# Attention of a gated layer: scores with tokens on the partitions, means and weight sums as extra columns, quads in a new order, and the first choice of tokens at six places of a quad

## The chip, the cores and the metric

One core of one Trainium2 chip runs the whole program. The metric is the device time of one execution in microseconds (us); lower is better. Tokens are handled in tiles of 128, one token per partition; a quad is four tiles (512 tokens), and there are 8 quads, q = 0 to 7, four for each of the two sequences of the batch (b = 0 and 1).

## What is computed

The reference, cut to its core (x is 2 x 2048 x 512, the context 2 x 77 x 512, 8 experts, each takes k = 512 tokens of each sequence, hidden size 2048, everything float32):

```python
xn = layernorm(x)
q, k, v = xn @ Wq.T + bq, ctx @ Wk.T + bk, ctx @ Wv.T + bv
attn = softmax(where(mask == 0, -inf, q @ k.T / sqrt(512)))
x = x + tanh(g_xattn) * (attn @ v @ Wo.T + bo)
xn = layernorm(x)
probs = softmax(xn @ gate_w.T)            # per token, over 8 experts
g, m = top_k(probs.transpose(0, 2, 1), k) # per sequence and expert
h = gelu(xn[m] @ w1) @ w2                 # per expert
x = x + tanh(g_ffn) * scatter_add(g * h)
```

## The kernel before

The program is written out per engine, with counting semaphores between the engines; each engine runs its own list in order, so the order of the code is the order of the work. It has four parts.

**Weights folded** (`prep_pe`, `prep_out`). Keys times Wq, the mean of each column taken off, become `qkc`, with 77 score columns and 8 router columns (JE = 85) per sequence; values times Wo become `vo` (77 x 512) and, times the router, `vg` (77 x 8). Part 0 is what the scores need, part 1 the rest.

**Attention, quad by quad** (`attention_pe`, `attention_act`, `attention_pool`, `attention_dve`). For a quad PE transposes the four tiles of x (L552), ACT copies them out as `xT` (L641), PE multiplies `qkc` (stationary, 85 columns) with `xT` (512 columns moving) into scores with the tokens on the free axis (L572), ACT copies them out as `sT` (L661), and PE turns them back so that tokens are on the partitions (L602). DVE scales and adds the mask bias (L793, four instructions), copies the router columns (L798), takes the largest score (L800) and its negative (L801). ACT takes four exponentials, whose row sums come out by its accumulator (L670). PE transposes them (L561), ACT copies them out as `eT` (L649). PE multiplies `eT` with `vo` (L590) and `vg` (L592), tile by tile, in turn. DVE multiplies by the reciprocal row sum (L764) and adds x (L770, "weigh"), then takes mean and variance of the new row (L817, L820), and POOL normalizes (L692 to L739). `logits_out` (L751 to L755) forms the router's logits. The spread of x comes from DVE for the first three quads, later from ACT: sum, mean, squares (L616, L620, L627). The quads overlap by one: in iteration `it`, PE does the transposes of x and the scores of quad `it`, and the rest of quad `it - 1`; DVE puts the score work of quad `it` between the second and the third weigh of quad `it - 1`.

**Choice** of 512 of 2048 tokens per expert, by a search over the bits of the threshold (`choice_dve`, `choice_pe`): 10 pieces of the same kind, each of which gets the counts of the piece before from PE (L886, L890), makes seven new thresholds (L895) and compares all probabilities with them (L899), after which PE counts (L962); then a piece for what lies above and at the threshold (L912 to L923), and a piece for the places (L930 to L942). Piece 0 also forms the probabilities. For b = 0 the function `between` lays the pieces beside the attention. Before, it does so from iteration `CHOOSE_FROM` = 5 on, at 3 places per iteration; all that is left runs in iteration 8. Then come `hot_dve` and `slots_dve` (L1366 to L1386) and `slots_pe` (L1355), which give the rows to fetch, POOL fetches them (L1419), PE transposes them (L1437), and ACT and DVE split them in two parts (L1442, L1452).

**Experts.** Expert 0 is plain (`hidden_pe` L1185, `output_pe` L1325); beside its first sequence DVE runs the second choice (b = 1). The other seven run products in a seven-product form (L1211). This part is the same in both kernels.

```python
        CHOOSE_FROM, PLACES = QB + 1, 3
...
            def between(it, place):
                at = (it - CHOOSE_FROM) * PLACES + place
                if it == NQ and place > 0:
                    pieces = range(at, N_PIECES) if place == 1 else ()
                else:
                    pieces = range(at, at + 1) if 0 <= at < N_PIECES else ()
```

## Time and profile before

| | us |
|---|---|
| three runs: median (lowest to highest) | 1578.08 (1573.19 to 1578.4) |
| the profiled execution: its time | 1578.86 |
| the profiled execution: its span | 1577.1 |
| first matmul of expert 0 (L1185), from the span's start | 183.18 |
| PE busy over the span | 1498.4 (95%) |
| DVE busy over the span | 1023.2 (65%) |

The profile's first part gives busy time per engine, the second cuts the span into 40 slices. In the first seven slices (0 to 276 us) PE is at 6 to 8 tenths, and after them at 9 and more. The chain that ended last is on PE for 85% of the span; the views by stage and by instruction, below, are of the part that lies ahead of the experts.

### The profile page before, as it was taken

How to read it: one execution, taken by the hardware profiler on the slowest of the kernel's cores; microseconds unless marked ns; L12 is line 12 of the kernel's file. 1: busy time of each engine (PE TensorE's matmuls, PEld its weight loads, DVE VectorE, ACT ScalarE, POOL GpSimd, SP SyncE). 2: the span in 40 equal slices, each digit the busy share in tenths (PEclk: the TensorE clock that was granted, in tenths of full speed). 3: DMA queues.
4: the chain of work that ended last, by engine and by line, in shares of the span. 5: the costliest groups of instructions: out<-in, count | busy, mean ns of one | idle time of the engine just before them, and what ended most of it. 6: DMA issues, size and time to landing. Idle time of an engine off the chain costs nothing.

```text
span 1577.1 us, 22321 instructions
## 1 busy us (share of the span) xinstructions
PE 1498.4 (95%) x7169; PEld 1214.6 (77%) x7169; DVE 1023.2 (65%) x1729; ACT 733.6 (47%) x1347; POOL 574.8 (36%) x541
## 2 busy tenths in 40 slices
PE   6887688999999999999999999999999999999996
PEld 5654467787788888888888888888888888888885
DVE  2578777557766767575766667667667665766642
ACT  1384233345444544455445454455445444554432
POOL 2266512453453144432443144404432344323311
PEclk9998799999999999999999999999999999999999
DMA  6175522553432443244323424244334423342133
GB/s 227 59 259 191 161 79 64 137 154 89 90 96 80 94 107 100 89 87 102 107 85 83 110 79 127 57 105 90 99 93 87 115 81 107 81 107 81 40 81 67
DMA packets 101401, 163.58 MB, mean 104 GB/s; under 512 B 7411, under 2 KB 45315, under 8 KB 101285
## 3 DMA queue, kind: packets, MB, share of 16 engines
q1 hardware_dynamic: 86885, 128.50, 26.1%
q0 software_dynamic: 14400, 33.56, 11.5%
q8 instruction: 69, 1.13, 0.3%
q14 instruction: 47, 0.39, 0.1%
HBM read 128.48 MB, written 33.55 MB: 103 GB/s over the span
## 4 chain that ended last, share of the span: by engine, by line
PE 85%; DVE 8%; ACT 2%; issue 2%; POOL 1%; DMA 1%; POOLq 0%; SPq 0%; DVEq 0%; ACTq 0%
PE bank L1325 42%; PE bank L1211 33%; PE bank L1185 4%; PE bank L1480 1%; PE bank L572 1%; PE bank L590 1%; DVE w2hl L1170 1%; PE bank L400 1%; DVE count L852 1%; DVE st L817 1%; DVE onehot L1366 1%; DVE atleast L899 1%; ACT xT L641 1%; DVE sc L793 0%; PE bank L1355 0%
## 5 line engine op out<-in xcount | busy, mean ns | idle before, releaser
L1325 PE MATMUL bank<-w2hl,hh 128*128 128x512 f32 x2048 | 637.8, 393 | 0.0
L1211 PE MATMUL bank<-xo,whl 128*128 128x512 f32 x2352 | 545.1, 390 | 4.8 <-DVE mix L1275 2.8
L1211 PEld LDWEIGHTS bank<-xo,whl 128*128 128x128 f32 x2352 | 441.8, 188 | 100.3 <-DVE mix L1275 3.7
L1325 PEld LDWEIGHTS bank<-w2hl,hh 128*128 128x128 f32 x2048 | 381.7, 189 | 76.5
L1325 PE MATMUL bank<-w2hl,hid_low 128*128 128x512 f32 x1024 | 399.8, 390 | 0.0
L1325 PEld LDWEIGHTS bank<-w2hl,hid_low 128*128 128x128 f32 x1024 | 192.8, 188 | 40.4
L1430 POOL DMA_INDIRECT layer_out<-y,slot_row x64 | 102.8, 1606 | 302.1 <-ACT y L1345 287.3
L1170 DVE TENSOR_TENSOR w2hl<-raw,w2hl 128x512 fp32r<-128x512 f32 x226 | 160.5, 731 | 53.0 <-ACT w2hl L1165 44.1
L1139 POOL TENSOR_TENSOR whl<-raw,whl 128x512 fp32r<-128x512 f32 x56 | 81.6, 1456 | 262.1 <-ACT whl L1105 262.1
L1165 ACT ACTIVATE w2hl<-raw 128x512 fp32r<-128x512 f32 x228 | 136.6, 625 | 58.1 <-DMA raw<-in_L_ffn_w 39.4
L1144 POOL TENSOR_TENSOR whl<-wsum,whl 128x512 fp32r<-128x512 f32 x56 | 75.1, 1340 | 183.6 <-ACT whl L1126 183.6
L1250 ACT ACTIVATE mix<-bank 128x512 f32<-128x512 f32 x56 | 33.3, 595 | 199.7 <-PE bank L1211 199.3
L1257 ACT ACTIVATE hid<-bank 128x512 f32<-128x512 f32 x56 | 33.5, 598 | 158.0 <-PE bank L1211 158.0
L1278 DVE TENSOR_TENSOR mix<-bank,mix 128x512 f32<-128x512 f32 x56 | 38.7, 692 | 101.3 <-PE bank L1211 99.3
L1185 PE MATMUL bank<-xp,whl 128*128 128x512 f32 x384 | 94.7, 397 | 1.7 <-DVE xp L1452 1.7
L1303 DVE TENSOR_TENSOR hid_low<-hid,hh 128x512 fp32r<-128x512 f32 x112 | 86.5, 778 | 12.8 <-ACT hh L1298 12.8
L1275 DVE TENSOR_TENSOR mix<-bank,mix 128x512 f32<-128x512 f32 x56 | 38.5, 688 | 80.8 <-PE bank L1211 80.5
L1185 PEld LDWEIGHTS bank<-xp,whl 128*128 128x128 f32 x384 | 73.6, 192 | 18.1 <-DVE xp L1452 2.4
L1133 POOL TENSOR_TENSOR whl<-raw,whl 128x512 fp32r<-128x512 f32 x32 | 46.9, 1485 | 105.9 <-ACT whl L1101 105.9
L1291 DVE TENSOR_TENSOR hid_low<-hid,hh 128x512 fp32r<-128x512 f32 x112 | 79.9, 713 | 0.5 <-ACT hh L1266 0.4
L1283 DVE TENSOR_TENSOR hid<-bank,mix 128x512 f32<-128x512 f32 x56 | 38.7, 691 | 63.5 <-PE bank L1211 63.4
L1146 POOL TENSOR_TENSOR whl<-wsum,whl 128x512 fp32r<-128x512 f32 x56 | 76.4, 1364 | 0.0
(224 smaller groups left out, 1771.8 us busy)
## 6 DMA issues: line engine op xcount, KB each, us to landing
raw<-in_L_ffn_w SPq DMA_DIRECT2D x228, 256.0 KB, 2.7
raw<-in_L_ffn_w SPq DMA_DIRECT2D x72, 512.0 KB, 4.8
x_s<-in_x SPq DMA_DIRECT2D x8, 1024.0 KB, 7.0
layer_out<-x SPq DMA_DIRECT2D x8, 1024.0 KB, 8.9
xn_rows<-xn SPq DMA_DIRECT2D x8, 1024.0 KB, 4.8
raw_k<-in_L_xattn_Wk SPq DMA_DIRECT2D x1, 1024.0 KB, 5.1
raw_q<-in_L_xattn_Wq SPq DMA_DIRECT2D x1, 1024.0 KB, 11.2
raw_v<-in_L_xattn_Wv SPq DMA_DIRECT2D x1, 1024.0 KB, 13.4
```

What stands on the lines that cost most here:

```text
L1133: last = pool.tensor_tensor(low[:, 4 * half:4 * half + 4, :].rearrange("p i f -> p (i f)"), raw1[:, p % 2, 2 * half:2 * half + 2, :].rearr ...
L1139: pool.tensor_tensor(low[:, 2 * A11:2 * A11 + 4, :], raw1[:, p % 2, :, 0:P], high[:, 2 * A11:2 * A11 + 4, :], ALU.subtract)
L1144: pool.tensor_tensor(low[:, 2 * S1:2 * S1 + 4, :], wsum[:, 0:4, :], high[:, 2 * S1:2 * S1 + 4, :], ALU.subtract)
L1146: pool.tensor_tensor(low[:, 2 * S3:2 * S3 + 4, :], wsum[:, 4:8, :], high[:, 2 * S3:2 * S3 + 4, :], ALU.subtract).then_inc(w1_low, 1)
L1165: act.activation(w2hl[:, f % 4, HIGH, :], raw2[:, slot, :], ACT.Copy).then_inc(w2_high, 1)
L1170: eng.tensor_tensor(w2hl[:, f % 4, LOW, :], raw2[:, slot, :], w2hl[:, f % 4, HIGH, :].bitcast(F32), ALU.subtract).then_inc(w2_low_early if ...
L1185: last = pe.matmul(H_BANKS[f % 2][:, :], whl[:, p % 2, part, 2 * k + f % 2, :], xp[:, b, xpart, k, :], start=(k == 0 and part == HIGH and ...
L1211: last = pe.matmul(bk[:, :], whl[:, p % 2, part, 2 * w + k, :], xo[:, xpart, x, k, :], start=(not adds and k == 0 and part == HIGH and xpa ...
L1291: dve.tensor_tensor(hid0_low[:, f % 4, :], hid0[:, f % 4, :], hh[:, f % 4, :].bitcast(F32), ALU.subtract)\
L1303: dve.tensor_tensor(hid1_low[:, f, :], hid1[:, f, :], hh[:, s % 4, :].bitcast(F32), ALU.subtract)\
L1325: last = pe.matmul(Y_BANKS[c][:, :], high if hpart == HIGH else low[:, c * P:(c + 1) * P], w2hl[:, f % 4, part, :], start=(s == 0 and hpar ...
L1430: pool.indirect_dma_start(out_rows, bass.IndirectOffsetOnAxis(ap=slot_row[:, b, c:c + 1], axis=0), y[:, c, :], None, compute_op=ALU.add).t ...
```

## The change

Scores: `score` takes `xT` of a tile as the stationary operand and `qkc` as the moving one, so that tokens come out on the partitions; `sT`, its copy and its turn back go. `qkc` gets an 86th column of -1/512, whose product is minus the mean of x (`xg1[..., E]`), and ACT's sums and `xmean` go; `vg` gets a ninth column of ones, whose product is the row sum of the exponentials, and the reciprocal is taken from that. DVE subtracts the largest score itself (`sm`), and ACT takes one exponential per quad. The banks for transposed tiles are two, before three; those for scores two, before one.

Order: per quad q, PE does the scores of quad q + 1 around the turn of the exponentials of q, then `route`, four `weigh_pe`, and the transposes of x of quad q + 2. DVE finishes quad q before it begins the score work of q + 1. The choice begins with quad 4 (`CHOOSE_FROM` = 4), with 6 places per quad; `hot_dve` and `slots_dve` are pieces 12 and 13. POOL fetches the first rows ahead of its work on quad 6.

```diff
-        T_BANKS = (2, 3, 4)
+        T_BANKS = (2, 3)
         O_BANKS = (bank[0], bank[1])
-        CHOOSE_FROM, PLACES = QB + 1, 3
+        SC_BANKS = (bank[6], bank[4])
+        CHOOSE_FROM, PLACES = QB, 6
...
+        def score(pe, q, i):
+            if i == 0:
+                wait(pe, mean_ready, q - 1)
+                wait(pe, sc_ready, q - 1)
+            pe.wait_ge(turn_out, turn_at["x", q, i] + 1)
+            for k in range(KD):
+                last = pe.matmul(SC_BANKS[q % 2][:, i * JM:(i + 1) * JM], xT[:, q % 2, k, i * P:(i + 1) * P],
+                                 qkc[:, k, q // QB, :], start=(k == 0), stop=(k == KD - 1))
+            if i == Q - 1:
+                last.then_inc(scored, 1)
+        def turn_e(pe, q):
+            pe.wait_ge(exped, q + 1)
...
+        def route(pe, q):
+            pe.wait_ge(turn_out, turn_at["e", q, 0] + 1)
+            wait(pe, rinv_ready, q)
+            for i in range(Q):
+                last = pe.matmul(VG_BANK[:, i * EM:(i + 1) * EM], eT[:, q % 2, i * P:(i + 1) * P], vg[:, q // QB, :],
+                                 start=True, stop=True)
+            last.then_inc(routed, 1)
+        def weigh_pe(pe, q, i):
+            n = Q * q + i
+            wait(pe, added, n - 1)
+            pe.matmul(O_BANKS[n % 2][:, :], eT[:, q % 2, i * P:(i + 1) * P], vo[:, q // QB, :],
+                      start=True, stop=True).then_inc(weighed, 1)
...
+            for q in range(NQ):
+                if q + 1 < NQ:
+                    score(pe, q + 1, 0)
+                    between(q - 1, 5)
+                    score(pe, q + 1, 1)
+                turn_e(pe, q)
+                if q + 1 < NQ:
+                    score(pe, q + 1, 2)
+                    score(pe, q + 1, 3)
+                between(q, 0)
+                route(pe, q)
+                weigh_pe(pe, q, 0)
+                weigh_pe(pe, q, 1)
+                between(q, 1)
+                weigh_pe(pe, q, 2)
+                between(q, 2)
+                weigh_pe(pe, q, 3)
+                for i in range(Q):
+                    if q + 2 < NQ:
+                        turn_x(pe, q + 2, i)
+                    if i == 0:
+                        between(q, 3)
+                    if i == 2:
+                        between(q, 4)
...
+            for q in range(NQ):
+                exps(q)
+                e_out(q)
+                if q == CHOOSE_FROM:
+                    choice_act(act, 0)
+                if LEAD <= q + 1 < NQ:
                     for i in range(Q):
+                        square(q + 1, i)
+                if q + 2 < NQ:
                     for i in range(Q):
+                        x_out(q + 2, i)
...
-                if it == NQ:
-                    w1_low_pool(pool, 0, 0, 0)
+                if it == NQ - 1:
                     for c in range(NC):
                         gather_pool(pool, 0, 0, c)
+                if it == NQ:
                     promote_pool(pool, 0, 0)
+                    w1_low_pool(pool, 0, 0, 0)
...
+            router_in(0)
+            prep_out(dve, prep_dve, False, 1, own)
+            for q in range(NQ):
+                softmax_in(q)
+                if q >= 1:
+                    logits_out(q - 1)
+                if q == CHOOSE_FROM:
+                    choice_start_dve(dve, own, 0)
+                if q + 1 < NQ:
+                    router_in(q + 1)
+                between(q, 0)
+                weights_in(q)
+                weigh(q, 0)
+                between(q, 1)
+                weigh(q, 1)
+                weigh(q, 2)
+                between(q, 2)
+                weigh(q, 3)
+                stats(q, (0,))
+                between(q, 3)
+                stats(q, (1, 2))
+                between(q, 4)
+                stats(q, (3,))
+                moments(q)
+                between(q, 5)
+            for c in range(NC):
                 split_tokens_dve(dve, 0, c)
             logits_out(NQ - 1)
...
+            def between(q, place):
+                at = (q - CHOOSE_FROM) * PLACES + place
+                if 0 <= at < N_PIECES + 2:
+                    do(at)
+            return between
```

`softmax_in` is the four instructions with the mask bias, the largest score and the subtraction, after waits for the scores, for POOL's factor and for the bias; `router_in` copies the nine columns out; `weights_in` copies the router's part out and takes the reciprocal of the ninth column.

The program's order of instructions shows two places. The first is DVE in a quad without a piece of the choice, from the first weigh on. Before (`sc` are the masked scores, `st` and `mv` the statistics of the new rows, `lg` the logits' steps):

```order
L770 SCALAR_TENSOR_TENSOR x<-bank,rinv,x_s 128x512 x2
L793 SCALAR_TENSOR_TENSOR sc<-bank,norm,mbias 128x77 x4
L798 COPY xg<-bank 128x32
L800 TENSOR_REDUCE smax<-sc 128x4
L801 TENSOR_SCALAR smaxn<-smax 128x4
L770 SCALAR_TENSOR_TENSOR x<-bank,rinv,x_s 128x512 x2
L817 BN_STATS st<-x 128x6 x4
L820 BN_AGGR mv<-st 128x2 x4
```

And in the changed program:

```order
L798 SCALAR_TENSOR_TENSOR x<-bank,rinv,x_s 128x512 x4
L807 BN_STATS st<-x 128x6 x4
L812 BN_AGGR mv<-st 128x2 x4
L752 SCALAR_TENSOR_TENSOR sc<-bank,norm,mbias 128x77 x4
L758 TENSOR_REDUCE smax<-sc 128x4
L760 TENSOR_TENSOR sm<-sc,smax 128x308
L775 TENSOR_TENSOR lg<-lgv,rinv 128x32
L777 TENSOR_TENSOR lg<-lg,xg 128x32
L779 TENSOR_TENSOR logits<-lg,norm 128x32
L769 COPY xg<-bank 128x36
L786 COPY lgv<-bank 128x32
L787 RECIPROCAL rinv<-bank 128x4
```

The score work of the next quad stood between the second and the third weigh; now it stands behind the statistics, and right ahead of the same quad's weigh.

The second place is PE in quad 4 of the changed program, from the second half of the scores of quad 5 on (L976 counts for the choice, L575 is `route`, L582 `weigh_pe`, L547 the transposes of x of quad 6):

```order
L558 MATMUL bank<-qkc,xT 128x86 x8
L976 MATMUL bank<-atleast,ones_m 128x56 x16
L575 MATMUL bank<-vg,eT 128x9 x4
L582 MATMUL bank<-vo,eT 128x512 x2
L976 MATMUL bank<-atleast,ones_m 128x56 x16
L582 MATMUL bank<-vo,eT 128x512
L976 MATMUL bank<-atleast,ones_m 128x56 x16
L582 MATMUL bank<-vo,eT 128x512
L547 MATMUL bank<-ident,x_s 128x128 x4
L976 MATMUL bank<-atleast,ones_m 128x56 x16
```

And DVE in the same quad, from the end of piece 0 to the last weigh:

```order
L913 TENSOR_TENSOR atleast<-prob,cand 128x896
L786 COPY lgv<-bank 128x32
L787 RECIPROCAL rinv<-bank 128x4
L798 SCALAR_TENSOR_TENSOR x<-bank,rinv,x_s 128x512
...
L913 TENSOR_TENSOR atleast<-prob,cand 128x896
L798 SCALAR_TENSOR_TENSOR x<-bank,rinv,x_s 128x512 x2
...
L913 TENSOR_TENSOR atleast<-prob,cand 128x896
L798 SCALAR_TENSOR_TENSOR x<-bank,rinv,x_s 128x512
```

Three counts of the choice now stand on PE ahead of `route`, of the third and of the fourth weigh of the same quad, and each waits for a comparison (`atleast`) on DVE; before, an iteration had one count ahead of the third weigh, one ahead of the transposed exponentials and one within the scores.

## Rows read from the trace of the kernel before

**Rows 1.** Busy time by engine, share of the span, instructions.

```profile
PE 1498.4 (95%) x7169; PEld 1214.6 (77%) x7169; DVE 1023.2 (65%) x1729; ACT 733.6 (47%) x1347; POOL 574.8 (36%) x541
```

**Rows 2.** Busy time per engine in stretches; last but two, PE's granted clock.

```profile
56.10:183.20 127.10, 93.92 (x581) 55.57 (x579) 92.23 (x257) 66.66 (x195) 67.67 (x94) 0.89 0.56 187
...
57.00:104.00 47.00, 42.99 (x196) 24.37 (x195) 28.71 (x82) 31.97 (x101) 24.04 (x36) 1.00 0.59 198
...
120.00:140.00 20.00, 16.35 (x121) 8.73 (x120) 17.49 (x51) 13.62 (x41) 12.96 (x17) 1.00 0.67 233
140.00:160.00 20.00, 12.49 (x98) 8.00 (x97) 16.44 (x40) 4.43 (x13) 13.06 (x16) 0.74 0.41 152
160.00:180.00 20.00, 6.62 (x69) 4.79 (x67) 13.64 (x39) 2.25 (x3) 6.48 (x11) 0.66 0.52 164
```

**Rows 3.** Timeline, DVE, at 56 us: start, us, engine, line, [idle before <-releaser].

```profile
55.94 0.17 DVE L460 COPY vg<-bank 77x16 f32<-77x16 f32 x1 [0.36 <-PE bank L432]
```

**Rows 4.** Timeline, DVE, one quad without choice.

```profile
98.40 0.75 DVE L770 SCALAR_TENSOR_TENSOR x<-bank,rinv,x_s 128x512 f32<-128x512 f32 x1 [1.95 <-PE bank L590]
...
100.05 0.90 DVE L793 SCALAR_TENSOR_TENSOR sc<-bank,norm,mbias 128x77 f32<-128x77 f32 x4
...
101.21 0.47 DVE L800 TENSOR_REDUCE smax<-sc 128x4 f32<-128x308 f32 x1
...
103.11 2.46 DVE L817 BATCH_NORM_STATS2 st<-x 128x6 f32<-128x512 f32 x4
105.61 0.38 DVE L820 BATCH_NORM_AGGREGATE mv<-st 128x2 f32<-128x6 f32 x4
```

**Rows 5.** Timeline, PE and ACT, from one quad to another two later.

```profile
70.08 0.59 ACT L649 ACTIVATE eT<-bank 77x512 f32<-77x512 f32 x1
...
92.80 0.63 PE L561 MATMUL bank<-ident,ex 128*77 128x128 f32 x4
93.50 0.59 ACT L649 ACTIVATE eT<-bank 77x512 f32<-77x512 f32 x1
93.76 3.63 PE L572 MATMUL bank<-xT,qkc 128*85 128x512 f32 x8 [0.34 <-ACT xT L641]
...
97.24 1.02 PE L590 MATMUL bank<-vo,eT 128*128 128x512 f32 x2
98.09 0.28 PE L592 MATMUL bank<-vg,eT 128*128 128x8 f32 x2
```

**Rows 6.** Timeline, PE: small matmuls with loads of 128 and of 77 columns.

```profile
42.19 4.44 PE L400 MATMUL bank<-ctxT,wvT 128*128 128x154 f32 x32 [1.45 <-ACT wvT L455]
...
54.69 1.21 PE L432 MATMUL bank<-qkc,voT 128*77 128x8 f32 x16
```

**Rows 7.** Timeline, ACT and DVE: exponential and subtraction of 128 columns.

```profile
108.78 0.29 DVE L864 TENSOR_TENSOR prob<-logits,pstat 128x128 f32<-128x128 f32 x1
...
109.11 0.31 ACT L856 ACTIVATE pexp<-prob 128x128 f32<-128x128 f32 x1 [3.31 <-DVE prob L864]
```

**Rows 8.** Timeline: a piece of the choice on DVE, then PE's count.

```profile
131.74 0.20 DVE L886 SCALAR_TENSOR_TENSOR found<-bank,cand 128x56 f32<-128x56 f32 x1
...
133.53 2.46 DVE L817 BATCH_NORM_STATS2 st<-x 128x6 f32<-128x512 f32 x4
133.67 0.59 PE L962 MATMUL bank<-atleast,ones_m 128*128 128x56 bf16 x16 [0.47 <-DVE atleast L899]
```

**Rows 9.** Timeline, DVE: the first choice's end.

```profile
162.37 0.21 DVE L886 SCALAR_TENSOR_TENSOR found<-bank,cand 128x56 f32<-128x56 f32 x1
...
167.70 2.29 DVE L1366 TENSOR_TENSOR onehot<-iota_slot,slot_lo 128x2048 bf16<-128x2048 bf16 x1
```

**Rows 10.** Timeline: PE at half clock, first fetch, first matmul of expert 0.

```profile
154.23 2.05 PE L590 MATMUL bank<-vo,eT 128*128 128x512 f32 x2 [0.33 <-issue]
...
172.77 1.14 POOL L1419 DMA_INDIRECT xg<-xn_rows,next_row  x1 [12.26 <-DVE next_row L1386]
...
183.18 6.17 PE L1185 MATMUL bank<-xp,whl 128*128 128x512 f32 x18 [1.72 <-DVE xp L1452]
```

More of the change, by code:

```diff
@@ L512, in prep_out @@
                 elif name == "vg":
[L513 removed]
+                    last = copy(vg[0:J, :, 0:E], bk[0:J, 0:B * E].rearrange("p (b e) -> p b e", b=B))
                 last.then_inc(mine, 1)
@@ L516, in prep_out @@
                     lead_stats_dve(eng, own, LEAD_AT[name, i])
-        turns = []
-        for it in range(NQ + 1):
-            turns += [("x", it, i) for i in range(Q) if it < NQ]
-            turns += [("e", it - 1, 0)] if it >= 1 else []
-            turns += [("s", it, 0)] if it < NQ else []
+        turns = [("x", q, i) for q in range(2) for i in range(Q)]
+        for q in range(NQ):
+            turns += [("e", q, 0)]
+            turns += [("x", q + 2, i) for i in range(Q) if q + 2 < NQ]
@@ new lines, in pe_bank_free, with turn_x @@
+            wait(pe, turn_out, turn_at[turn] - 1)
+        def turn_x(pe, q, i):
+            if i == 0:
+                pe.wait_ge(x_in[q % 3], 16 * (q // 3 + 1))
+            pe_bank_free(pe, ("x", q, i))
+            for k in range(KD):
+                last = pe.transpose(turn_bank(("x", q, i))[:, k * P:(k + 1) * P],
+                                    x_s[:, q % 3, i, k * P:(k + 1) * P], ident[:, :])
+            last.then_inc(turned, 1)
+        def score(pe, q, i):
[3 more added lines that the diff above has]
+            pe.wait_ge(turn_out, turn_at["x", q, i] + 1)
+            for k in range(KD):
+                last = pe.matmul(SC_BANKS[q % 2][:, i * JM:(i + 1) * JM], xT[:, q % 2, k, i * P:(i + 1) * P],
+                                 qkc[:, k, q // QB, :], start=(k == 0), stop=(k == KD - 1))
+            if i == Q - 1:
+                last.then_inc(scored, 1)
@@ L679, in first_deviations @@
                 s = q % 2
+                wait(pool, sc_ready, q - 1)
                 if q < LEAD:
@@ L824, in attention_dve, with stats, moments @@
-            for c in (0, 1):
+            def stats(q, tiles):
+                if tiles[0] == 0 and q >= 1:
+                    dve.wait_ge(x1_stats, q)
+                for i in tiles:
+                    dve.wait_ge(added, Q * q + i + 1)
+                    own.mark(dve.bn_stats(st2[:, i, :], x1[:, q % 2, i, :]))
+            def moments(q):
+                dve.wait_ge(dve_own, own.n)
+                for i in range(Q):
+                    last = dve.bn_aggr(mv2[:, q % 2, i, :], st2[:, i, :])
+                    own.mark(last) if i < Q - 1 else last.then_inc(x1_stats, 1)
@@ new lines, in attention_dve @@
+            router_in(0)
+            prep_out(dve, prep_dve, False, 1, own)
+            for q in range(NQ):
+                softmax_in(q)
[20 more added lines that the diff above has]
+                between(q, 5)
@@ L870, in step @@
                 dve.wait_ge(dve_own, own.n)
-            if b == 0 and piece == 0:
-                choice_start_dve(dve, own, 0)
             if piece == 0:
@@ L978, in beside_attention, with first_choice_dve, do, first_choice_pe @@
         def beside_attention(do):
-            def between(it, place):
-                at = (it - CHOOSE_FROM) * PLACES + place
-                if it == NQ and place > 0:
-                    pieces = range(at, N_PIECES) if place == 1 else ()
-                else:
-                    pieces = range(at, at + 1) if 0 <= at < N_PIECES else ()
-                for piece in pieces:
-                    do(0, piece)
-            return between
+            def between(q, place):
[3 more added lines that the diff above has]
+            return between
+        def first_choice_dve(dve, own):
+            def do(piece):
+                if piece < N_PIECES:
+                    choice_dve(dve, own, 0, piece)
+                elif piece == N_PIECES:
+                    hot_dve(dve, 0, 0)
+                else:
+                    slots_dve(dve, 0, 0)
+            return do
+        def first_choice_pe(pe):
+            def do(piece):
+                if piece < N_PIECES:
+                    choice_pe(pe, 0, piece)
+                elif piece == N_PIECES:
+                    slots_pe(pe, 0)
+            return do
         H_BANKS = (bank[4], bank[5])
@@ L1825, in _ @@
             pool.memset(mean_m[:, :], 1.0 / D).then_inc(consts, 1)
+            for b in range(B):
+                pool.memset(qkc[:, :, b, JE:JM], -1.0 / D).then_inc(tails, 1)
+                pool.memset(vg[:, b, E:EM], 1.0).then_inc(tails, 1)
             pool.wait_ge(pool_start, 4)
@@ L1857, in _ @@
             attention_act(act)
-            act.wait_ge(scored, NQ)
+            for c in range(NC):
+                first_tokens_act(act, c)
             for f in range(2):
@@ L1862, in _ @@
             w1_high_act(act, 0, 0, 1)
-            for c in range(NC):
-                first_tokens_act(act, c)
             choice_act(act, 1)
```

320 lines of the change are left out of this document (113 added, 207 removed).

## The prediction

> **What bounds the kernel now.** I read the busy times first: PE works 95% of the span [rows 1], and the experts, where it is full, are the same program in both kernels. So only the time from the start to the first matmul of expert 0, at 183.18 us [rows 10], can change, and whatever moves that matmul moves the end by as much. Next the stretches: from 56.1 to 183.2 us PE is busy 93.92 of 127.1 us and DVE 92.23 [rows 2]; neither is full. In the quads without choice PE is nearly so (42.99 of 47 us), and the work repeats every 11.7 us: the transposed exponentials are copied out at 70.08 and, two quads later, at 93.50 [rows 5]. From quad 4 on DVE has three pieces of the choice to a quad, and after 140 us PE falls to 12.49 and 6.62 of 20 us and is granted its faster clock only for part of it [rows 2]. So what counts is how the engines wait for one another, and I follow one quad after the other through the new order, by durations of the trace. I take 0.05 us from one engine's end to the next one's start, and from the start of a `vo` product to the DVE work on it 1.14 us (97.24 to 98.40, and 0.86 us of it is PE's own time) [rows 4, 5].
>
> **Start.** The folding of the weights is the same work. The changed PE does the first scores and the second quad's transposes ahead of part 1 instead of behind it, and waited there for copies anyway; I leave its end at 56.1 us, where DVE copies `vg` [rows 3]. PE's work up to there counts at nothing because those waits cover it; if they don't, it costs up to 2 us.
>
> **A quad without choice, before 11.7 us.** I set t = 0 where DVE begins `softmax_in`.
> - DVE: the masked scores take 0.90, the largest 0.47 [rows 4]. The subtraction of 308 elements isn't in the trace; it lies between the same with 128 elements, 0.29 [rows 7], and a 512-element weigh, 0.75 [rows 4]; I take 0.48. With the gaps DVE is through at 1.96.
> - ACT: one exponential of 308, between 0.31 for 128 [rows 7] and 0.59 for 512 [rows 5]; 0.46, to 2.46. PE turns from 2.5; ACT's copy starts 0.70 after PE, as in [rows 5], and ends at 3.8.
> - PE in the meantime does two tiles of the next quad's scores, 16 instructions with 128 columns loaded and 86 moved. They are bounded by 0.076 us each (8 columns moved, 77 loaded) and by 0.139 (154 moved, 128 loaded) [rows 6]; the loads are full size, so I take 0.12, 0.95 a tile. PE is free at 4.85. All four tiles cost 3.8 against 3.63 before [rows 5]; only the turn back and the copy of `sT` are saved. `route` is 8 more such instructions, to 5.8.
> - DVE weighs at 6.94 (5.8 + 1.14) and 7.9; the third product needs the first bank, so it is weighed at about 8.96, the fourth at 9.84, to 10.6. Then 2.46 and 0.38 for the statistics [rows 4]: 13.4.
> This chain passes DVE, ACT, PE, ACT, PE and DVE again with nothing put beside it, because the score work of the next quad no longer stands between two weighs. ACT and POOL are busy for about half of the stretch, 66.66 and 67.67 of 127.1 us [rows 2], and ACT for less after the change; its saved sums and three exponentials count at nothing, since it waits in any case. A quad costs 13.4 for 11.7.
>
> At the scores the Trainium skill has a rule ("TensorE: Matmul & The Clock Gate", "LDWEIGHTS (loading the stationary operand)"): a load takes its columns divided by 1.2 nanoseconds, 107 ns for 128, however few columns then move. It speaks against this change, which now loads 128 columns for every 86. By it the two tiles that stand in the chain would take 1.7 us in place of my 1.9 and the sum would be 1 us less over the quads; the trace's 0.139 us with 128 columns is near it.
>
> **A quad with six pieces.** A piece is 1.8 us on DVE (131.74 to 133.53), a count 0.6 on PE [rows 8]. Quad 4:
> - To 2.6 as above, with `logits_out`, then the choice's start; `router_in` must wait for the scores, 5.2. Piece 0 with its probabilities is 2.2 us, to 7.5. PE counts to 8.2, and only then does `route`, to 9.15: DVE waits until 10.3 for the first weigh, 11.05.
> - Piece 1 to 12.85, second weigh to 13.55. PE was free, but its third product stands behind the count of piece 1, from 13.5: weighed at 14.65, to 15.35.
> - Piece 2 to 17.15; count, fourth product from 17.8: weighed at 18.95. DVE waits 1.8 us with nothing to do. To 19.65.
> - Statistics and pieces 3, 4 and 5 follow without a wait: 28.0.
> Quad 5 the same, with pieces 6 to 9, then 5.3 us for the last two, 162.37 to 167.70 [rows 9]: 29.1. Quad 6: the one-hot matrices (`hot_dve`, 2.29 us [rows 9] and two small ones, 3.0) are ahead of `slots_pe` and `route`: first weigh at 10.9, end at 17.8. POOL fetches from 12.3 on, while the quad goes on. Before, expert 0 began 10.4 us after the first fetch, at 172.77 [rows 10]; that latency is now hidden. Quad 7 has no scores behind the exponentials: weighed from 5.9, statistics to 12.3; then four splits, of which the last two wait for two banks (PE, ACT, DVE in turn), 15.9. There expert 0 begins.
>
> **Sum.** 56.1 + 4 x 13.4 + 28.0 + 29.1 + 17.8 + 15.9 = 200.5, against 183.2: 17.3 us later. DVE's own work in it is about 98 us (92.23, and 6 for subtraction, copies and the moved first scores), so it would wait 46 of 144 us, where before it waited 35 of 127.
>
> **PE's clock.** Before, PE was granted 0.74 of full speed where it was busy 12.49 of 20 us, and 0.66 where 6.62 [rows 2]; at the half clock (1.2 GHz) a `vo` product of 1.02 us took 2.05 [rows 10]. In quads 4 and 5 of my walk PE is busy 14 of 28 us, in pieces with pauses of up to 3 us. In its chain stand, per quad, turn and scores 2.3, `route` 0.95, three products 2.6 and about 1 for the counts: nearly 7 us, that double at the half clock; 5 in quad 6. So this costs between 0 and 19 us. As the pauses are shorter than those of before, I take a third, 6 us.
>
> 17.3 + 6 = 23 us. The profiled execution took 1578.86 us (0.8 over the median of the runs): 1578.9 + 23 = 1602 us.
>
> **The rivals.**
> - The half clock holds through the choice. For it: the pauses recur four times a quad. Against it: from 120 to 140 us, with PE busy 16.35 of 20 us and choice pieces beside it, the clock stayed full [rows 2]. Price 19 in place of 6: 1615 us. The Trainium skill has this as a rule (same page, "HAM oscillation — how this bites in real kernels"): a program that pauses between short bursts begins every burst slow. By that, this rival would be the forecast.
> - Slower by little: full clock, score matmuls at 0.076 us each (0.7 us off the chain in eight places), a quicker handing over. 17.3 less 6 gives 11 us: 1590.
> - No change: the loss in quads 0 to 3 (6.8 us) stays, but the choice loses nothing, because its pieces fill DVE's waits. What DVE waits in quads 4 and 5 (about 7 us each) would have to go. 1582 us.
> - Faster: DVE, not the chain, sets the time. It decides as soon as DVE's waits from 56 us on fall under 29 us (127.1 - 98). One quad's pieces would have to run while PE is in the turn and the products of the same quad. If DVE never waited, expert 0 would begin at 154 and the time be 1550; halfway to my walk's 200.5 it is 1573. For it: 35 us of idle DVE time exist, and the fetch is hidden. Against it: the order of PE has three counts ahead of three products of the same quad, and PE's matmuls keep their order.
>
> **How the numbers follow.** A measurement here tells about 0.5% from no change, 7.9 us. The forecast (some loss of clock, 1592 to 1610) 0.50; half clock, 1610 and more, 0.20; slower by little 0.15; no change 0.08; faster 0.07. So slower 0.85, same 0.08, faster 0.07. The range takes the first and the third case whole and the half clock to 1620: 1586 to 1620.
>
> **What would show it.** Right: in the changed profile DVE's first weighs of quads 1, 2 and 3 are 13 to 14 us apart, in quads 4 and 5 about 28; DVE waits 1 to 2 us for PE at the third and the fourth weigh of these; the first matmul of expert 0 lies at 200 us or later, and behind it the distances are as before. Wrong: quads without choice at 12 us or less, or choice quads under 24 us, or that matmul before 183 us. A clock of 1.00 from 110 to 190 us would take the 6 us away, one near 0.5 would give the first rival.

## The result, and the profile after

The changed kernel took 1620.68 us, the median of 4 runs (1619.94 to 1621.75); the kernel before 1576.49 us, the median of its 4 (1573.19 to 1578.4). The ratio is 1.0287, with a 95% interval of 1.0266 to 1.0307: slower, as forecast, but by 44 us in place of 23, and 0.7 us outside the range. The profiled execution took 1620.17 us with a span of 1618.3; before, 1578.86 and 1577.1.

The first part of the changed kernel's page, against [rows 1]:

```profile
PE 1523.5 (94%) x7329; PEld 1246.7 (77%) x7329; DVE 1028.0 (64%) x1738; ACT 709.6 (44%) x1238; POOL 568.9 (35%) x545
```

The span grew by 41.2 us. Where it grew is read from the first and last start of one line's matmuls. In the answer for the plain product of expert 0 (L1205 now, L1185 before) and the one for the seven-product form (L1231 now, L1211 before), the two numbers behind the comma are those starts; first before, then after:

```profile
L1185 PE MATMUL bank<-xp,whl x384: 387/389/796, 183.2 to 380.4; 128*128 128x512 f32 x192
L1211 PE MATMUL bank<-xo,whl x2352: 387/389/628, 383.5 to 1510.3; 128*128 128x512 f32 x196
```

```profile
L1205 PE MATMUL bank<-xp,whl x384: 388/389/796, 219.1 to 417.4; 128*128 128x512 f32 x192
L1231 PE MATMUL bank<-xo,whl x2352: 387/389/636, 420.6 to 1551.5; 128*128 128x512 f32 x196
```

Expert 0 begins 35.9 us later (219.1 for 183.2), the second expert 37.1 later, and the last matmul of L1231 41.2 later. So 36 us were lost ahead of the experts, and 5.3 in a part that is the same in both kernels. The first loss is 18.6 us more than the walk of the prediction gave it, the second was not in it at all.

The quads of the changed kernel, cut where DVE begins `softmax_in`; the last stretch ends with the first matmul of expert 0 (us, the busy time of PE, PEld, DVE, ACT and POOL with its count, last but two the granted clock):

```profile
55.44:68.61 13.17, 11.98 (x81) 9.21 (x80) 8.01 (x22) 3.23 (x6) 2.04 (x2) 1.00 0.09 18
68.61:86.36 17.75, 15.51 (x70) 11.68 (x70) 8.49 (x27) 3.23 (x6) 8.07 (x12) 0.71 0.51 175
86.36:99.50 13.14, 10.81 (x70) 8.03 (x70) 8.48 (x26) 6.16 (x14) 7.86 (x12) 1.00 0.49 180
99.50:117.16 17.66, 15.41 (x70) 11.60 (x70) 8.47 (x27) 6.16 (x14) 8.17 (x13) 0.71 0.69 219
117.16:147.77 30.61, 18.17 (x143) 12.60 (x143) 20.10 (x54) 6.57 (x15) 9.56 (x15) 0.75 0.51 167
147.77:178.44 30.67, 22.43 (x193) 17.10 (x192) 20.14 (x61) 6.37 (x14) 8.51 (x13) 0.69 0.25 89
178.44:199.80 21.36, 12.37 (x54) 8.39 (x53) 11.73 (x32) 3.98 (x10) 8.09 (x11) 0.68 0.24 71
199.80:219.10 19.30, 11.26 (x37) 6.57 (x37) 10.93 (x30) 5.09 (x9) 10.63 (x19) 0.70 0.70 248
```

Quads 0 and 2 ran at a full clock and took 13.17 and 13.14 us, where the walk had 13.4. Quads 1 and 3 hold the same work (70 matmuls each in quads 1, 2 and 3), were granted 0.71 of the clock and took 17.75 and 17.66. So the order costs 1.5 us a quad against the 11.7 of before, and the clock 4.5 more in every second one. Quads 4 and 5 took 30.6 and 30.7 for the walk's 28.0 and 29.1, quad 6 took 21.4 for 17.8, and the last stretch 19.3 for 15.9.

The timeline of DVE in quad 1, from the copy of the router columns to the last weigh, and then the same in quad 2:

```profile
75.64 0.20 DVE L769 COPY xg<-bank 128x36 f32<-128x36 f32 x1 [4.50 <-PE bank L558]
77.22 0.19 DVE L786 COPY lgv<-bank 128x32 f32<-128x32 f32 x1 [1.38 <-PE bank L575]
...
79.22 0.75 DVE L798 SCALAR_TENSOR_TENSOR x<-bank,rinv,x_s 128x512 f32<-128x512 f32 x1 [1.72 <-PE bank L582]
80.83 0.75 DVE L798 SCALAR_TENSOR_TENSOR x<-bank,rinv,x_s 128x512 f32<-128x512 f32 x1 [0.86 <-PE bank L582]
...
91.32 0.20 DVE L769 COPY xg<-bank 128x36 f32<-128x36 f32 x1 [2.43 <-PE bank L558]
92.15 0.19 DVE L786 COPY lgv<-bank 128x32 f32<-128x32 f32 x1 [0.63 <-PE bank L575]
...
93.21 1.51 DVE L798 SCALAR_TENSOR_TENSOR x<-bank,rinv,x_s 128x512 f32<-128x512 f32 x2 [0.78 <-PE bank L582]
```

Each wait of DVE for PE about doubles: 4.50 for 2.43, 1.38 for 0.63, 1.72 for 0.78. They are the links of the chain that the prediction named (turn, scores, `route`, product), and with nothing beside them DVE pays PE's slower pace in full.

In quad 4, DVE at the third and fourth weigh (L798), and PE's counts (L976) of the same quad:

```profile
133.35 0.75 DVE L798 SCALAR_TENSOR_TENSOR x<-bank,rinv,x_s 128x512 f32<-128x512 f32 x1 [1.28 <-PE bank L582]
138.80 0.75 DVE L798 SCALAR_TENSOR_TENSOR x<-bank,rinv,x_s 128x512 f32<-128x512 f32 x1 [2.89 <-PE bank L582]
```

```profile
131.47 0.59 PE L976 MATMUL bank<-atleast,ones_m 128*128 128x56 bf16 x16 [1.85 <-DVE atleast L913]
131.89 1.42 PE L582 MATMUL bank<-vo,eT 128*128 128x512 f32 x2
135.96 0.93 PE L976 MATMUL bank<-atleast,ones_m 128*128 128x56 bf16 x16 [2.65 <-DVE atleast L913]
136.71 2.05 PE L582 MATMUL bank<-vo,eT 128*128 128x512 f32 x2
```

The two engines take turns: PE waits 2.65 us for DVE's comparison with a product behind it that was ready, then DVE waits 2.89 for the product. The last product came at the half clock (2.05 us for two instructions), so the 1.8 us foreseen at the fourth weigh became 2.9.

What PE waited for over the whole span (engine, line, <- releaser: us, times, longest), the first rows of the changed kernel:

```profile
PE bank L976 <- DVE atleast L913: 18.6, 9, 2.6
PE bank L567 <- ACT ex L644: 17.2, 7, 6.0
...
PE bank L1231 <- issue: 4.9, 4, 1.3
```

Before, the corresponding wait for comparisons was 10.0 us in 6 and a wait for exponentials was not among the rows; the row with "issue" had no counterpart either. It stands in the experts' loop:

```profile
764.90 1.75 PE L1231 MATMUL bank<-xo,whl 128*128 128x512 f32 x7
767.77 4.40 PE L1231 MATMUL bank<-xo,whl 128*128 128x512 f32 x18 [1.12 <-issue]
```

PE does seven matmuls of a pass of the loop and then stands still for 1.12 us, with no semaphore to wait for. This happens four times, 4.9 us in all, and they cover what this line lost: of the 5.3 us, 4.1 lie between the first and the last start of this line (1130.9 us for 1126.8), and the other 1.2 in expert 0.

### The profile page after: what moved, and what is told of

Same layout as the page of the kernel before. It is cut to its first block, busy times and chain, and to the rows that moved or that the text cites. A ratio compares the mean times of both kernels' runs of the same rounds, so it can differ in the third digit from the quotient of the medians.

```text
span 1618.3 us, 22526 instructions
## 1 busy us (share of the span) xinstructions
PE 1523.5 (94%) x7329; PEld 1246.7 (77%) x7329; DVE 1028.0 (64%) x1738; ACT 709.6 (44%) x1238; POOL 568.9 (35%) x545
## 4 chain that ended last, share of the span: by engine, by line
PE 85%; DVE 9%; issue 2%; ACT 2%; DMA 1%; POOL 0%; POOLq 0%; SPq 0%; DVEq 0%; ACTq 0%
PE bank L1345 40%; PE bank L1231 32%; PE bank L1205 3%; PE bank L582 2%; PE bank L1502 1%; PE bank L558 1%; DVE st L807 1%; DVE atleast L913 1%; DVE w2hl L1190 1%; PE bank L399 1%; DVE count L868 1%; PE bank L575 1%; DVE onehot L1386 1%; DVE cand L909 0%; PE bank L567 0%
## 5 line engine op out<-in xcount | busy, mean ns | idle before, releaser
L1231 PE MATMUL bank<-xo,whl 128*128 128x512 f32 x2352 | 545.5, 390 | 8.4 <-issue 4.9
L1231 PEld LDWEIGHTS bank<-xo,whl 128*128 128x128 f32 x2352 | 441.2, 188 | 104.8 <-issue 8.2
L1185 ACT ACTIVATE w2hl<-raw 128x512 fp32r<-128x512 f32 x228 | 136.4, 624 | 58.7 <-DMA raw<-in_L_ffn_w 41.7
L1277 ACT ACTIVATE hid<-bank 128x512 f32<-128x512 f32 x56 | 33.5, 598 | 163.7 <-PE bank L1231 163.7
L1205 PE MATMUL bank<-xp,whl 128*128 128x512 f32 x384 | 96.3, 402 | 1.4 <-DVE xp L1474 1.4
L1205 PEld LDWEIGHTS bank<-xp,whl 128*128 128x128 f32 x384 | 74.6, 195 | 17.5 <-DVE xp L1474 1.7
## 6 DMA issues: line engine op xcount, KB each, us to landing
raw_v<-in_L_xattn_Wv SPq DMA_DIRECT2D x1, 1024.0 KB, 13.4
```

What stands on the lines that cost most here:

```text
L1185: act.activation(w2hl[:, f % 4, HIGH, :], raw2[:, slot, :], ACT.Copy).then_inc(w2_high, 1)
L1205: last = pe.matmul(H_BANKS[f % 2][:, :], whl[:, p % 2, part, 2 * k + f % 2, :], xp[:, b, xpart, k, :], start=(k == 0 and part == HIGH and ...
L1231: last = pe.matmul(bk[:, :], whl[:, p % 2, part, 2 * w + k, :], xo[:, xpart, x, k, :], start=(not adds and k == 0 and part == HIGH and xpa ...
```

## The experiments

**Theories.** A, the order on PE: counts ahead of ready products, and no softmax work between weighs, make a chain that nothing covers. B, the clock: the chain would be bearable if PE kept 2.4 GHz. C, six places or the early start of the choice are at fault by themselves. D, the stop in the experts comes from where the loop lies in PE's program. The kernel before took 1575.53 us beside the first four runs and 1575.92 beside the next four. "Front" below is the first matmul of expert 0, "rest" the span from there to its end: 183.2 and 1393.9 before, 219.1 and 1399.2 after. Front and rest come from one profiled execution each, and each time but the last two is a single run.

The front also holds the folding of the weights, which most edits leave alone and which still ends at different times: the 32 matmuls at 15 to 16 us took 6.50 us in the change and 4.44 with the counts behind, and no trace here says why. So the table counts the attention from a mark that all kernels have, the start of DVE's copy of `vg` [rows 3]; the walk had 144.6 us from there.

| kernel | `vg` copied | expert 0 | between | rest |
|---|---|---|---|---|
| before | 55.9 | 183.2 | 127.2 | 1393.9 |
| the change | 55.3 | 219.1 | 163.7 | 1399.2 |
| counts behind | 52.7 | 197.4 | 144.7 | 1399.3 |
| softmax between | 54.0 | 203.8 | 149.8 | 1399.0 |
| both | 55.6 | 181.2 | 125.5 | 1398.2 |
| idle matmuls | 53.2 | 201.9 | 148.7 | 1394.4 |
| three places | 55.2 | 222.0 | 166.8 | 1396.5 |
| eight small matmuls | 55.4 | 218.9 | 163.5 | 1392.7 |
| late softmax, idle matmuls | 53.4 | 194.5 | 141.1 | 1390.5 |
| late softmax | 55.8 | 180.0 | 124.2 | 1390.9 |
| the same again | 53.2 | 177.8 | 124.6 | 1393.9 |
| scores first | 55.6 | 180.9 | 125.4 | 1391.8 |

**Counts behind the products (A).** PE's first three counts of a quad each go behind the product that they stood ahead of.

```diff
-                between(q, 0)
                 route(pe, q)
                 weigh_pe(pe, q, 0)
                 weigh_pe(pe, q, 1)
+                between(q, 0)
+                weigh_pe(pe, q, 2)
                 between(q, 1)
-                weigh_pe(pe, q, 2)
+                weigh_pe(pe, q, 3)
                 between(q, 2)
-                weigh_pe(pe, q, 3)
```

> The changed kernel with one thing else: in PE's list each count of the choice at the places 0, 1 and 2 stands behind the product that it stood ahead of. Theory (order and clock): DVE no longer waits at the first, third and fourth weigh of quads 4 and 5; by the walk at full clock this is 5.2 us in each of the two and 2 in quad 6, 12 us, and some 8 more because PE's part of the chain there also ran at half clock: first matmul of expert 0 at about 200 in place of 219.7 us, time about 1600. Rival (the places of the counts don't matter, DVE waits for something else): no change, 1620.

Measured 1598.77 us: 22 less than the change. The front is at 197.4, the rest 1399.3. From the mark it is 19.0 us less: that is what three places a quad had on PE ahead of the products cost, half of the 36.5 us lost there.

**Softmax work between two weighs (A).** `softmax_in` of quad q + 1 moves from behind the statistics to between the second and the third weigh of quad q, the place that it had in the kernel before.

```diff
-            for q in range(NQ):
-                softmax_in(q)
+            softmax_in(0)
+            for q in range(NQ):
...
                 weigh(q, 1)
+                if q + 1 < NQ:
+                    softmax_in(q + 1)
                 weigh(q, 2)
```

> The changed kernel with DVE's four score instructions, largest score and subtraction of quad q + 1 put back between the second and the third weigh of quad q, where they stood before. Theory: the chain DVE, ACT, PE, ACT, PE of a quad again runs beside the statistics of the quad before; quads 0 to 3, now 61.7 us together, take about 47 (11.7 each), and PE keeps the full clock there; 15 to 25 us in all, time 1595 to 1605. Rival (the new form of the scores costs by itself, not the order): quads stay at 13 and more, time above 1612.

Measured 1604.64: 16 less. The front is at 203.8, the rest 1399.0. The quads without choice now take 11.6 to 13.1 us (ends of the statistics at 73.15, 84.72, 97.81 and 110.88), not the 11.7 expected: `softmax_in` stands ahead of the third weigh, and there DVE waited 2.54 us for POOL's factor and, a quad later, 2.87. From the mark the edit gives 14 us.

**Both (A).** The two edits together.

> Both edits of order together: counts behind the products, score work of the next quad between two weighs. Theory: DVE becomes the bound of quads 4 and 5 (about 20 us each), quads without choice take 11 to 12 us; expert 0 begins at 175 to 185 us, time 1575 to 1585, so about the kernel before. If the six places were the fault in themselves, it would stay above 1600.

Measured 1581.38. The front is at 181.2, 2 us ahead of the kernel before; the rest is 1398.2, with the stops in the loop (3.7 us in 4). From the mark the two edits alone gave 19 and 14, which add to 33, and together they gave 38.2. So the order accounts for all of the 36.5 that was lost ahead of the experts. The granted clock from 100 to 180 us was only 0.81, with DVE busy most of the time:

```profile
100.00:180.00 80.00, 57.47 (x450) 41.13 (x447) 65.48 (x179) 22.77 (x50) 41.95 (x61) 0.81 0.55 181
```

DVE is busy 65.48 of 80 us in it; in the kernel before it was 64.26. That the clock matters little when DVE is this full is argued; no run holds the clock in this order.

**Idle matmuls that keep the clock (B).** Ahead of each turn of the exponentials PE does six matmuls whose result is overwritten, and ahead of each count eight. The order of the change stays.

```diff
+        def warm(pe, bk, n):
+            for _ in range(n):
+                pe.matmul(bk[:, 0:P], ident[:, :], mean_m[:, :], start=True, stop=True)
...
+                pe_bank_free(pe, ("e", q, 0))
+                warm(pe, turn_bank(("e", q, 0)), 6)
                 turn_e(pe, q)
```

> The changed kernel with idle matmuls added on PE where it waits (6 of 128 x 128 ahead of each turn of the exponentials, 8 ahead of each count of the choice), whose results nobody reads. Theory (the half clock is what the walk at full clock lacks): granted clock 1.00 nearly throughout from 56 to 200 us, quads 0 to 3 at 13.2 us each, expert 0 begins at about 201 in place of 219.7, time about 1601. Rival (the clock is a symptom, the waits come from elsewhere): time 1620 or, with the matmuls in the way, more.

Measured 1598.33: 22 less. Stretches of it:

```profile
56.00:100.00 44.00, 41.13 (x275) 32.08 (x275) 25.96 (x76) 14.88 (x32) 19.82 (x31) 1.00 0.56 177
100.00:160.00 60.00, 53.43 (x509) 44.67 (x508) 42.08 (x106) 15.54 (x36) 21.15 (x30) 1.00 0.48 157
160.00:180.00 20.00, 18.67 (x165) 15.34 (x164) 12.85 (x42) 4.58 (x11) 8.10 (x12) 0.91 0.20 69
```

The clock is full to 160 us, all of quads 1 to 3 take 13.15 us (ends of the statistics at 66.91, 80.05, 93.20, 106.35), and the front is at 201.9. From the mark that is 15 us less than the change. With the 38.2 of the order that makes 53, more than the 36.5 there are: in part they are the same microseconds, since a chain that is covered does not feel the clock. In this kernel PE does not stop in the loop, and its rest is 1394.4.

The idle matmuls did not hold the clock to the end. The last stretch, from the `softmax_in` of quad 7 to expert 0, is as long as in the change (19.05 for 19.30 us):

```profile
182.85:201.90 19.05, 11.02 (x36) 6.72 (x36) 10.98 (x30) 5.05 (x9) 10.99 (x19) 0.74 0.68 236
```

So the full-clock walk is tested up to there: it had 128.5 us from the first `softmax_in` to that of quad 7, and this kernel took 129.5, the change 144.4.

**The choice as before, three places from quad 5 on (C).** The pieces run at places 1, 3 and 4 of quads 5 to 7, the remaining ones behind quad 7, and the fetch behind them, as in the kernel before; all else is the change.

```diff
-        CHOOSE_FROM, PLACES = QB, 6
+        CHOOSE_FROM, PLACES = QB + 1, 3
...
+                elif q >= CHOOSE_FROM and place in (1, 3, 4):
+                    do((q - CHOOSE_FROM) * PLACES + (1, 3, 4).index(place))
```

> The changed kernel with the six places undone: the choice begins with quad 5, three pieces per quad (behind the first weigh, and between the statistics), the last three search pieces (9 and on), one-hot matrices and fetch behind quad 7, as before the change. Theory: six places are not the fault in themselves. Quads 5 to 7 get about 19, 19 and 17 us, the tail 21: at full clock 200 us to expert 0, the same as with six places, with the same loss of clock 212 to 222 us; time 1612 to 1625. Rival (the early, dense choice is what costs): time under 1605.

Measured 1620.39, no gain; the front is at 222.0. The last statistics end at 198.1 in place of 215.7, but 23.9 us then pass before expert 0, in place of 3.4, for the rest of the choice and the fetch. So undoing the six places and the early start gains nothing, with the order otherwise kept. It is the sum of two things, though: only one count a quad is left ahead of a product, and in return PE waits 5.66 us for the choice's last step and 4.98 for the fetched rows, which six places had hidden.

**Eight small matmuls at PE's start (D).** Eight matmuls of eight columns, whose result is overwritten, in part 0 of the folding, where PE waits in any case. All that lies behind them moves in PE's program.

```diff
                 pe.wait_ge(consts, 1)
+                for _ in range(8):
+                    pe.matmul(bank[6][0:8, 0:8], ident[:, 0:8], ident[:, 0:8], start=True, stop=True)
```

> The changed kernel with eight tiny matmuls (8 columns) put at the start of PE's program, where it waits for the first data. In the profile after the change PE stops for 1.0 to 1.3 us seven matmuls into each pass of the rolled loop over experts, with nothing that it waits for ('issue', 4.9 us in four passes), and before the change it doesn't. Theory: this is the fetch of PE's program behind the branch, and depends on where the loop's head lies in it; 32 more instructions ahead of the loop move it, the stops go, and the time falls by 4 to 5 us to about 1616. Rival (the stops come from the data or from other engines): they stay, 1620 or 1621.

Measured 1613.66, about 7 us less for eight matmuls more. Its L1233 is L1231 of the change:

```profile
L1233 PE MATMUL bank<-xo,whl x2352: 387/389/628, 420.6 to 1544.8; 128*128 128x512 f32 x196
```

```profile
765.10 7.19 PE L1233 MATMUL bank<-xo,whl 128*128 128x512 f32 x31
```

The loop is reached at 420.6 us as in the change, and left 6.7 us earlier; the stop after seven matmuls is gone. The kernels that have it (the change, counts behind, softmax between, both, three places; 3.3 to 4.9 us in four stops) have rests of 1396.5 to 1399.3; the other seven 1390.5 to 1394.4, one of them with two short stops of 0.9 us together. The first and the last start of this line show it with less scatter: 1128.6 to 1130.9 us apart with the four stops, 1122.7 to 1126.8 without. So the stop hangs on what lies ahead of the loop in PE's program, its position there; nothing in the loop itself was changed. The stops are 4.9 us and the loop is 6.7 shorter; what the other 1.8 are is open. That it is the fetch of instructions is not shown. The Trainium skill has such a mechanism ("Runtime: NRT & Kernel Launch", "Instruction fetch mechanics"): a taken branch to a target outside the window that the sequencer holds must wait for a fetch. The trace agrees in so far as the stop comes early in a pass and has no releaser; it does not show the fetch.

**Softmax work behind the last weigh, with both other cures.** `softmax_in(q + 1)` between the fourth weigh and the statistics, the counts behind the products, and lighter idle matmuls (four and six).

> Counts behind the products; score work of quad q + 1 between the last weigh of quad q and its statistics (between the second and third weigh it waited 2.9 us for POOL's factor in quads 2 and 3 of the run with both edits); and the idle matmuls, 4 ahead of each turn and 6 ahead of each count. Theory: quads 2 and 3 at 11.7 us in place of 13.1, full clock in quads 4 to 6, expert 0 at about 170 in place of 181.2, time 1565 to 1572, under the kernel before. Rival (DVE is full, nothing more to gain): as with both edits, 1581.

Measured 1586.87, a miss by 15 us. The front is at 194.5, although the granted clock was 0.94 from 104 to 180 us. PE in quad 4 (L587 are the idle matmuls, L1002 the counts, L822 the weigh):

```profile
111.01 1.60 PE L587 MATMUL bank<-mean_m,ident 128*128 128x128 f32 x12 [2.44 <-DVE x L822]
112.45 0.58 PE L1002 MATMUL bank<-atleast,ones_m 128*128 128x56 bf16 x16
...
115.88 2.01 PE L587 MATMUL bank<-mean_m,ident 128*128 128x128 f32 x12 [1.91 <-DVE x L822]
```

The idle matmuls needed a bank that the weigh frees. They waited 2.44 us for it and ran 1.60 more, with a count behind them whose comparison was done, and DVE waited 2.11 and 2.19 us for the two counts. Filling PE's waits costs nothing only where the filler needs nothing itself.

**The same without idle matmuls, with the eight small ones at the start.**

> The same two edits of order without the idle matmuls, with the eight tiny matmuls at the start. Against the run before it this tells what the clock is worth once DVE is the bound. Theory: little is left on PE in DVE's chain, so 2 to 6 us; expert 0 at about 175, no stops in the rolled loop, time 1570 to 1575. Rival: the half clock costs here as much as in the changed kernel, time 1585.

Measured 1572.82. The front is at 180.0, the rest 1390.9. Compared with the miss, taking the idle matmuls out gave 16.9 us from the mark, at a lower clock (the eight small ones changed nothing there: 163.5 for 163.7):

```profile
56.00:104.00 48.00, 45.07 (x295) 34.12 (x294) 33.94 (x95) 19.16 (x42) 26.63 (x38) 1.00 0.57 187
104.00:140.00 36.00, 25.34 (x244) 17.66 (x244) 29.46 (x80) 9.80 (x24) 17.46 (x25) 0.86 0.53 177
140.00:180.00 40.00, 26.41 (x170) 18.66 (x169) 31.92 (x92) 11.35 (x23) 20.95 (x33) 0.79 0.63 208
```

In the quads without choice PE is busy 45 of 48 us and they take 10.9 to 11.5 us, little more than PE's own work; in the others DVE is busy 61 of 76.

**That kernel timed, and one with the scores ahead of the counts.** The only wait of DVE over 2 us in the choice quads of the kernel above was this one, with a second like it of 1.36 us:

```profile
131.24 0.20 DVE L771 COPY xg<-bank 128x36 f32<-128x36 f32 x1 [3.24 <-PE bank L560]
```

PE had the scores of the next quad behind counts that waited for DVE. The new order moves the counts of places 2 to 5 further back. Behind the last of the four transposes comes one tile of the scores, then the count of place 4, then the second tile. The counts of places 2 and 3 still stand between transposes, so it does less than the expectation names. DVE takes the router columns behind the first piece of the choice. PE's part, against the change:

```diff
                 for i in range(Q):
                     if q + 2 < NQ:
                         turn_x(pe, q + 2, i)
-                    if i == 0:
+                    if i == 1:
+                        between(q, 2)
+                    if i == 2:
                         between(q, 3)
-                    if i == 2:
-                        between(q, 4)
+                if q + 2 < NQ:
+                    score(pe, q + 2, 0)
+                between(q, 4)
+                if q + 2 < NQ:
+                    score(pe, q + 2, 1)
```

> The kernel of the run before (softmax work behind the last weigh, counts behind the products, eight small matmuls) again, timed in rounds against the kernel before the change: 1571 to 1574 us, a ratio of 0.996 to 0.999, if its one look was no accident; a ratio of 1 or more if it was.

> The kernel with the softmax work of the next quad behind the last weigh, the counts behind the products and the eight small matmuls, and two orders more: PE does all four transposes of x and the first two tiles of the scores ahead of the counts that it would have to wait for, and DVE takes the router columns of the next scores behind the first piece of a choice quad, where it waited 3.24 and 1.36 us for them. If DVE is what sets the choice quads now, those 4.6 us go: expert 0 near 176 us, about 1568 us. If PE's half clock sets them, at most 2 us go: 1571 to 1573.

Measured, against 1575.56 us for the kernel before (23 runs): the kernel of the run above 1574.06 (12 runs, 1569.47 to 1578.8), ratio 0.9992 with an interval of 0.9981 to 1.0003; the new order 1574.4 (11 runs), ratio 0.9993, 0.9984 to 1.0002. Neither can be told from the kernel before. The new order missed its 1568. The wait of 3.24 us is gone from it, but from the mark it takes 125.4 us, where the kernel without the new order took 124.2 and 124.6. (The fronts 180.0 and 177.8, of two executions of one program, differ by what lies ahead of the mark.) One wait grew in its place, between quads 6 and 7, where it had been 1.55 us:

```profile
170.06 0.21 DVE L785 TENSOR_TENSOR logits<-lg,norm 128x32 f32<-128x32 f32 x1 [3.55 <-POOL norm L698]
```

## Why the prediction was right, and where it was wrong

**What bounds it: right.** The loss came from the order in which the engines wait, ahead of the experts, and not from busy time: PE's grew by 25 us, some of it the same instructions at the half clock, and DVE's by 5.

**Quads without choice, 13.4 us: right at a full clock** (13.17 and 13.14). The estimated instructions came out as taken: the subtraction of 308 elements 0.48 us, the exponential 0.46, and the scores 1.92 us for 16, which is 0.12 each and 0.96 a tile, near the 0.95. The load rule of the Trainium skill ("TensorE: Matmul & The Clock Gate", "LDWEIGHTS (loading the stationary operand)"; 107 ns for 128 columns) would have been a little low; the measurement decides for 0.12. The full clock belongs to it: at 0.50, in quad 1, 16 of them took 3.55 us, 0.22 each.

**Quads with six pieces: right in mechanism.** The alternation at the third and fourth weigh is there, and moving the counts behind the products took 19.0 us away. With the clock held by idle matmuls the stretch up to the `softmax_in` of quad 7 took 129.5 us, for the walk's 128.5. That the whole front came so near to the walk (201.9 for 200.5) is in part luck: the folding ended 2.7 us early in that execution, and the last stretch took 3.2 us more than the walk had.

**PE's clock, "I take a third, 6 us": this is the step that failed.** Between the walk's 200.5 and the measured 219.1 lie 18.6 us. Up to the `softmax_in` of quad 7, idle matmuls that hold the clock take 14.9 us away (144.4 to 129.5): that much goes with the clock there, where 6 were taken for the whole front. The last stretch is 3.4 us over the walk in the change and 3.2 with the idle matmuls, at a granted 0.70 and 0.74. In the change its first weigh comes 8.3 us after `softmax_in`, for the walk's 5.9, behind a turn of 1.14 us and a `route` of 1.88, which took 0.66 and 0.99 at the full clock; so some 2 us of the 3.4 are the clock too, an estimate from these rows, and no run holds the clock in this stretch. Two things in the term were wrong. It held only for quads 4 to 6, but 9 us fell in quads 1 and 3, which have no piece of the choice (17.75 and 17.66 for 13.15); the walk had PE waiting in each of them and did not ask what that does to the clock. And the reason given for a third, "the pauses are shorter than those of before", is no measure: with pauses mostly of 2 to 3 us, and one of 6.0, the stretches from 120 to 220 us were granted 0.66 to 0.74. The rival "half clock holds" came near to the case, with 19 us. The Trainium skill's rule beside it ("TensorE: Matmul & The Clock Gate", "HAM oscillation — how this bites in real kernels"), by which a program that pauses between short bursts begins each burst slow, agrees with quads 1 and 3 and with the choice quads; it does not agree with quad 2, whose burst after the same pause of 1.99 us ran at 1.00. The argument against the rival, a full clock from 120 to 140 us with PE busy 16.35 of 20 us [rows 2], was from the old order; in the new one PE is busy 12.49 us of the same 20, at 0.74.

**"Whatever moves that matmul moves the end by as much": wrong by 5.3 us.** The part behind it is the same program, but not in the same place. PE's loop is 4.1 us longer, with 4.9 us of stops that eight matmuls at the start remove. The other 1.2 are in expert 0 and may be scatter: two executions of the late-softmax kernel differ by 3.8 us there (from 180.0 to 379.5, and from 177.8 to 381.1).

**Together.** 18.6 us of the front where 6 were taken is 12.6 too little, and the 5.3 behind make 17.9. The profiled execution is 1620.17, the forecast was 1602: 18.2. The direction came out for the reason given, the order; its size did not.

**The rival on the other side** (DVE sets the time) did not come in the change, but the experiments show how near it lay: with three counts and one block of DVE work in other places the same arithmetic gives a front of 180 us. It is not 154: in the quads without choice PE is then busy 45 of 48 us, which leaves little to win there.

**Open.** Why the clock falls in quads 1 and 3 and not in 2; how much of the last stretch is the clock; what makes the folding end up to 3 us apart, and expert 0 up to 4, from one execution to the next; and whether anything short of less work would bring the front much under 178.

## What to carry to other kernels

When two engines hand work back and forth, an instruction that waits must not stand in an in-order queue ahead of work that is ready; three such places cost 19 us here, and moving them is free. Compare stretches from a mark that both kernels have, since what lies ahead of it can scatter by microseconds. A chain with nothing beside it pays twice, since the pauses also cost TensorE its clock: price its instructions at the half clock unless the trace shows the full one with the same pauses. And compare the parts "that are the same" too: a loop further on may run differently because it lies elsewhere in the program.

## What was not expected of the hardware

In quad 1 the clock fell although PE was hardly idle. Stretches of the changed kernel:

```profile
56.00:70.00 14.00, 11.94 (x79) 9.01 (x77) 8.74 (x24) 3.23 (x6) 3.10 (x5) 1.00 0.17 46
70.00:72.00 2.00, 0.88 (x4) 0.88 (x5) 1.04 (x5) 0.46 (x1) 1.81 (x4) 0.78 0.92 264
72.00:80.00 8.00, 8.00 (x30) 6.18 (x28) 1.23 (x4) 0.59 (x1) 5.20 (x7) 0.50 0.66 249
```

From 72 to 80 us PE was busy all the time and granted 0.50; it had been busy 11.94 of 14 us before, and the pause ahead of it was 2 us. A pause that did nothing in quad 2 went with the half clock in quad 1, and PE then worked without a gap at half pace. Quad 3 repeats it from 104 to 112 us (0.50, busy 8.00 of 8). In the kernel with three places quad 4 is without choice too, and the lengths alternate on: 17.66, 13.14, 17.65 and 13.14 us for quads 1 to 4. What differs ahead of the three bursts is small: in the 14.0 us up to the end of the pause PE was busy 10.81 us at a granted 1.00 in quad 1, 10.82 at 0.99 in quad 3, and 11.75 at 0.77 in quad 2, where the half pace of the quad before had stretched its work. Whether that is the reason no run here shows. And eight small matmuls added at the start made the time of an unchanged loop, hundreds of microseconds later, 6.7 us shorter.
